# Two small subtractions of a gated attention block moved: one between the two halves of a reciprocal's refinement, one ahead of a wait

## The reference, cut to what matters

```python
emb = layernorm(x) + ctx
q, k, v = emb @ wq + bq, emb @ wk + bk, emb @ wv + bv
w = pos_bias * (|i - j| < 64)
ek, ew = exp(k - max(k)), exp(w - max(w))
num, den = ew @ (ek * v), ew @ ek
y = sigmoid(q) * num / den
attn = y @ wo + bo
a = layernorm(attn + emb) * gamma + beta
x1 = x + tanh(g_xattn) * (layernorm(relu(a @ w1 + b1) @ w2 + b2 + a) * gamma + beta)
xn = layernorm(x1);  xp = xn shifted by one row
xr, xk = mu_r * xn + (1 - mu_r) * xp, mu_k * xn + (1 - mu_k) * xp
out = x1 + tanh(g_ffn) * sigmoid(xr @ W_r) * (relu(xk @ W_k)**2 @ W_v)
```

## Time and profile before

| what | value |
|---|---|
| median of 3 runs | 456.14 us (455.56 to 456.22) |
| the profiled execution: its time, its span | 455.75 us, 454.0 us |
| PE busy | 434.3 us, 96% of the span |
| DVE, ACT, POOL busy | 377.5, 286.6, 290.7 us |
| granted TensorE clock, mean | 0.996 of full speed |

### The profile page before, as it was taken

The page is one execution under the profiler, slowest core; times in us unless marked ns, Lnnn a source line. Parts: engine busy times, 40 slices in busy tenths (PEclk is TensorE's granted clock), DMA queues, the critical chain, the costliest instruction groups (busy, mean ns, idle before and its releaser), DMA issues.

```text
span 454.0 us, 8151 instructions
## 1 busy us (share of the span) xinstructions
PE 434.3 (96%) x2892; PEld 394.7 (87%) x2892; DVE 377.5 (83%) x769; ACT 286.6 (63%) x453; POOL 290.7 (64%) x230
## 2 busy tenths in 40 slices
PE   8999989999869999999999999999999999999985
PEld 8888779989759898998889988998989998998975
DVE  5898878989778979799798978799778877678876
ACT  2682653848467487745968387745976387629373
POOL 2766848564578657894778747894677543773632
PEclk9999999999989999999999999999999999999999
DMA  8840401442215650438215651436213330011002
GB/s 272 286 139 3 140 29 42 138 131 69 92 66 153 189 150 15 139 100 239 92 48 156 194 142 33 140 101 190 94 48 103 95 119 22 1 48 47 3 0 94
DMA packets 43497, 47.23 MB, mean 104 GB/s; under 512 B 8512, under 2 KB 39744, under 8 KB 43456
## 3 DMA queue, kind: packets, MB, share of 16 engines
q1 hardware_dynamic: 42368, 45.13, 32.7%
q10 hardware_dynamic: 1088, 1.57, 1.0%
HBM read 30.76 MB, written 15.93 MB: 103 GB/s over the span
## 4 chain that ended last, share of the span: by engine, by line
POOL 31%; issue 25%; DVE 11%; ACT 6%; PE 4%; POOLq 0%; DVEq 0%; ACTq 0%
POOL ek_lo L242 5%; POOL ev_lo L242 5%; PE ps L1846 4%; POOL x_beta L650 3%; POOL xk_lo L242 3%; POOL emb L354 2%; POOL a_rows L650 2%; DVE xk L1062 2%; DVE ps L979 2%; DVE xr L1062 2%; POOL rs_fin L630 2%; POOL nmr_fin L633 2%; POOL rs_ff L630 1%; POOL rs_mid L630 1%; POOL ve_ff L621 1%
## 5 line engine op out<-in xcount | busy, mean ns | idle before, releaser
L1846 PE MATMUL ps<-w_hi,hid_hi 128*128 128x256 f32 x248 | 61.2, 284 | 0.9 <-ACT hid_hi L1800 0.9
L1846 PE MATMUL ps<-w_lo,hid_hi 128*128 128x256 f32 x248 | 60.8, 281 | 0.0
L242 POOL TENSOR_TENSOR ek_lo<-y,ek_hi 128x1024 fp32r<-128x1024 f32 x13 | 36.1, 2778 | 28.0 <-DVE xr L1062 25.7
L1621 ACT ACTIVATE hid_hi<-ps,b 128x512 fp32r<-128x512 f32 x60 | 37.7, 681 | 23.3 <-PE ps L1846 23.2
L1846 PE MATMUL ps<-a_hi,w_hi 128*128 128x512 f32 x128 | 50.7, 396 | 0.0
L1846 PE MATMUL ps<-a_hi,w_lo 128*128 128x512 f32 x128 | 50.7, 396 | 0.0
L1846 PEld LDWEIGHTS ps<-w_hi,hid_hi 128*128 128x128 f32 x248 | 46.7, 188 | 1.8 <-issue 1.4
L1846 PEld LDWEIGHTS ps<-w_lo,hid_hi 128*128 128x128 f32 x248 | 46.8, 189 | 0.4
L1139 DVE SCALAR_TENSOR_TENSOR hid_lo<-ps,neg_b,hid 128x512 fp32r<-128x512 f32 x60 | 41.3, 737 | 3.1 <-ACT hid L1627 3.0
L1627 ACT ACTIVATE hid<-hid_hi,neg_b 128x512 f32<-128x512 f32 x60 | 40.0, 722 | 0.0
L1846 PE MATMUL ps<-w_hi,hid_lo 128*128 128x256 f32 x248 | 36.0, 285 | 0.6
(11 more groups left out here) (287 smaller groups left out, 1413.6 us busy)
## 6 DMA issues: line engine op xcount, KB each, us to landing
x_in<-in_x SPq DMA_DIRECT2D x8, 512.0 KB, 5.3
emb<-in_ctx SPq DMA_DIRECT2D x8, 512.0 KB, 4.4
x_beta<-in_x SPq DMA_DIRECT2D x8, 512.0 KB, 4.2
out<-out_sb SPq DMA_DIRECT2D x7, 512.0 KB, 4.1
key_room<-norm SPq DMA_DIRECT2D x6, 512.0 KB, 2.6
y<-key_room SPq DMA_DIRECT2D x24, 128.0 KB, 2.9
fin_room<-xk SPq DMA_DIRECT2D x6, 512.0 KB, 2.6
out_sb<-fin_room SPq DMA_DIRECT2D x24, 128.0 KB, 2.9
```

Source lines behind the costliest of these rows:

```text
L242: eng.tensor_tensor(dst, src, f32(hi), ALU.subtract).then_inc(done, 1)
L1621: act.activation(tile(hi, b, T), bank(relu_pair(n, q), b), ACT.Relu, bias=b1[:, m:m + 1]).then_inc(hid_hi_done, 1)
L1846: return pe.matmul(o, s, m, start=start, stop=stop, skip_group_check=True)
```

## The change

Three things move, and nothing is added or removed.

1. `sums_low(i, 1)` on DVE goes from behind the whole refinement to between the two instructions of its second half (steps 2 to 7).
2. In step 2 alone (a = 0), POOL does `y_low(i)` ahead of its wait for `xr_done`. The wait itself stays, now in front of `xk_low`.
3. In step 2 alone, DVE does the row statistics of the batch two ahead (`head_stats(e)`) behind `turn_key_squares(d)` and no longer before `mix_k`.

```diff
                 if has(d):
                     emb_plus_bo(d, 1 - p)
+                if a == 0:
+                    y_low(pool, i)
                 pool.wait_ge(xr_done, DC * (a + 1))
-                y_low(pool, i)
+                if a > 0:
+                    y_low(pool, i)
                 xk_low(pool, a)
                 xr_low(pool, a)
...
-            def inverse(n, c):
+            def inverse(n, c, between=None):
...
                 dve.scalar_tensor_tensor(out=bank(0, c), in0=bank(1, c), scalar=-2.0, in1=tile(y, c, T),
                                          op0=ALU.mult, op1=ALU.mult).then_inc(den_read, 1)
+                if between is not None:
+                    between()
                 dve.wait_ge(den_read, DC * n + c + 1)
...
                 inverse(i, 0)
                 if a == 0:
                     turn_fin_squares(a)
-                inverse(i, 1)
-                sums_low(i, 1)
+                inverse(i, 1, lambda: sums_low(i, 1))
                 gate_inverse(i)
                 make_y(i)
                 if a == 0:
                     key_max(d)
-                    head_stats(e)
                 mix_k(a)
                 mix_r(a)
...
                 turn_key_squares(d)
+                if a == 0:
+                    head_stats(e)
                 attention_sum(i, p)
```

## The result

The changed kernel takes 453.69 us (median of 5 runs, 453.31 to 454.11), the kernel before 456.22 (5 runs beside them, 455.56 to 457.17). The ratio is 0.9942, with an interval of 0.9927 to 0.9957: faster by 2.0 to 3.3 us. The profiled execution has a span of 451.9 us and a time of 453.69.

The account below looks back on a forecast made before the run. PE was 96% busy, but a ring through mix, POOL and hidden layer also bounds each middle step. Gains 1.29 (step 2) + 0 (steps 3 to 6) + 0.27 (step 7) = 1.56 us from 455.75: 454.3 said, range 452.5 to 455.7.

Parts of the forecast that it names:

- POOL holds the mix: Steps 3 to 6: POOL's addition of `bo` keeps the mix from starting before 176.46, against 176.45 now; gain 0 per step.
- rival 1: Steps 3 to 6: POOL doesn't hold the mix, far sums give 1.56 us more, time 452.7; chance 0.17.
- Far sums, steps 3 to 6: 0: Moved subtraction removes PE's 0.39 us wait, but the gain is held at the mix: 0, ends +1.56 and -0.8.
- Steps 4 to 6 repeat step 3: Steps 4 to 6 have far-sum waits of 0.38 to 0.40 us and gain 0 each, like step 3.
- TensorE's limb: Middle steps: path from PE's numerator through gate product, mix and statistics to the hidden layer; level with POOL's to 0.01 us.
- Step 7: 0.27: Step 7: no next batch, so no `bo` addition on POOL; the mix starts earlier and the 0.27 us wait is gained.
- Step 2: 1.29: Step 2: earlier exponentials and square's high part bring DVE's norm transposes from 140.81 to 139.52, gaining 1.29 us.
- rival 2: Step 2: new PE waits of 2.2 and 1.3 us bring half-clock products, gain lost; time 455.8, chance 0.17.
- The level: Whole run: starting time for the forecast, the profiled execution's own 455.75 us, 0.39 below the median of three runs.
- rival 3: Steps 2 to 7: moved subtraction waits for ACT's copy and blocks the refinement; 457.7 us, chance 0.06.
- rival 4: Middle steps: DVE's L1090 comes before POOL's addition, letting 0.4 us through per step; time about 453, chance 0.07.

Follow-up runs that it names:

- the kernel with GpSimd's other order: The whole change, plus GpSimd's bias addition `finish_a` ahead of `ev_low`, against the kernel before: 452.34 us, ratio 0.9919.
- GpSimd's order: Only GpSimd's `finish_a` put ahead of `ev_low` in the kernel before, nothing else changed: 456.49 us, ratio 0.9994.

## Why the prediction was right, and where it was not

*The time.* 454.3 was forecast and 453.69 measured, inside the forecast's own range of 453.6 to 454.9. The mechanisms named were largely the right ones, but the total was helped by luck: the gain was forecast a microsecond too small, from a level half a microsecond too low.

*POOL holds the mix.* The forecast was right, and its rival 1 wrong. The mix was to start 176.06 - 170.05 = 6.01 us behind the refinement and came at 5.95. It was to be let go where it started before, and its third operation starts at 7.74, where it was 7.73. The Trainium skill (SBUF — State Buffer, section Who interferes with whom) has the second comer wait for the whole of the first. The trace agrees up to the last 0.19 us of GpSimd's recorded span, and the kernel with GpSimd's other order shows the gain released. One sign of the forecast didn't come: TensorE's waits for the hidden layer's low part were to grow from 0.5 to 0.9 us in a step, and whole-run they went from 2.4 to 2.6. What TensorE gains in steps 3 to 5 it loses earlier in the step, at VectorE's addition to the values (L871).

*Far sums, steps 3 to 6: 0.* Right for three steps, wrong for step 6, which kept 0.43. The step that failed is "Steps 4 to 6 repeat step 3". Step 6 has no ninth batch to prepare, and its period was 1.1 us shorter already. In the profile of before, ScalarE waits for TensorE there, and so does the hidden layer's sum:

```profile
344.01 1.06 ACT L1593 ACTIVATE ev_hi<-xk 128x1024 fp32r<-128x1024 f32 x1 [1.92 <-PE ps L1846]
...
354.99 1.29 DVE L1026 TENSOR_TENSOR res<-ps,a_rows 128x512 f32<-128x512 f32 x2 [1.62 <-PE ps L1846]
```

After the change both waits are still there:

```profile
342.14 1.06 ACT L1598 ACTIVATE ev_hi<-xk 128x1024 fp32r<-128x1024 f32 x1 [1.92 <-PE ps L1851]
...
353.12 1.29 DVE L1031 TENSOR_TENSOR res<-ps,a_rows 128x512 f32<-128x512 f32 x2 [1.61 <-PE ps L1851]
```

In this step TensorE's limb is the longer one; it has no wait for L871 either. The mix is held there too (its first operation takes 1.19 us), but it doesn't matter, and what TensorE saves counts. The kernel with GpSimd's other order bears this out: its mix of step 6 is hardly held (0.80 us for the first operation), and the step is no shorter (49.91).

*Step 7: 0.27.* It gave 0.29 to 0.34. Right.

*Step 2: 1.29.* Between the two first profiles it gave 1.02. The chain of the forecast is there (the mix by ScalarE's copies, the exponentials behind it, the statistics ahead of the attention sum). The term that was mis-sized is the moment of the copies: the forecast took the DMA as landed when they started before. ScalarE starts them 9.61 to 9.68 us behind the refinement in twelve of the 14 profiles, before and after, but at 9.98 in the first one of the changed kernel. That is 0.3 late, all of the 0.27 missing; the second profile, without it, gave 56.30, or 1.36. The 1.3 us wait for the attention sum was not seen at first, since slow products filled it (1.01 in the second profile). All this is measured from the profile that the forecast rests on; against the other kind of execution of the kernel before, the gain of step 2 is larger, as follows.

*Step 2 gives nothing (rival 2).* Wrong, but its clock was real and worked on the other side. The low stretch cost the kernel before, where TensorE was late, 0.96 more in its second execution than in the profiled one. Between the second profiles step 2 gave 58.60 - 56.30 = 2.30 us. So the medians differ by 2.5 where the first profiles, without the start, show 1.02 - 0.07 + 0.43 + 0.29 = 1.67. This is the term that the forecast had too small: it took the one profiled execution, with the short low stretch, for every execution, and about half of them have the long one, which the change takes away. That the low stretch makes up the rest of the 2.5 is shown by the pair of profiles and by the two groups of runs; no run varied the clock by itself.

*The level.* The forecast counted from 455.75, the time of the profiled execution, which was 0.2 to 0.9 below the medians of before. Its 1.56 taken from 456.22 would have been 454.66, a worse hit. The forecast was helped here by two errors of opposite sign: the gain was too small by about 1, the level too low by 0.5.

*Slower (rival 3).* The moved subtraction blocks nothing: DVE's next instruction starts 0.45 behind it in step 3, and no step got longer. *Overtaking (rival 4)* didn't occur: the large scalar_tensor_tensor (L1090, now L1095) keeps its median of 3.2 us.

## What to carry to other kernels

When two limbs of a loop are level to a hundredth, an edit to one of them gives nothing and says nothing about its worth: the far sums gave 0 us in three steps, GpSimd's order gave 0, and both together 1.2. Look for the step of the loop that differs from the others (here the last but one, with a batch less), and check its waits by itself before writing that it repeats the rest. Where a profile has an engine's pause followed by a lower granted clock, take a second profile before comparing stages: one execution can miss a microsecond of the cost that half of them have. The mean granted clock of the unprofiled runs tells how many are of each kind.

## What the runs showed of the hardware

- TensorE's clock fell to 0.50 (1.2 GHz) at pauses of 3.86 and 3.87 us in the kernels with the low output in its old place, and of 2.92, 2.69, 2.59 and 2.38 us in step 2, and not at pauses of 2.35, 1.65, 1.38, 1.37 and 1.33 us. Behind equal pauses it stayed low for 3.4 us in one execution and for 6.8 in another. In seven of nine profiles the lower level began inside the pause, in two 0.2 and 0.6 us behind its end, so that the pause's length alone doesn't say what it costs.
- The cost depends on who is late: about 1 us between the short and the long low stretch where ScalarE's relu waited for TensorE, 0.02 us between none and a short one where DVE was the path.
- A scalar_tensor_tensor of 128x512 with both tensors in SBUF that starts 0.66 us before the end of a GpSimd tensor_tensor stands still for 0.47 us; with 0.24 to 0.27 us left to that end it took 0.79 to 0.81 us against a median of 0.746.
- A DMA at one and the same place of the program was waited for until 9.61 to 9.68 us behind the step's first refinement in twelve profiles, and until 9.98 and 10.40 in two.
